# A slot-attention stage in which the context sums, the context norms and one wait change their beats

## What is computed

```python
Pn = rmsnorm(P, input_norm_w)                 # P is the context
k_proj = Pn @ Wk.T
v_proj = Pn @ Wv.T
for _ in range(NUM_ITERS):                    # 3
    sn = rmsnorm(slots, slot_norm_w)
    scores = einsum('bkd,bmd->bkm', sn @ Wq.T, k_proj) * SCALE
    attn = softmax(scores, axis=-2)
    attn = attn / (sum(attn, axis=-1, keepdims=True) + EPS)
    updates = einsum('bkm,bmd->bkd', attn, v_proj)
    slots = gru_cell(updates, slots, ...)
```

## Time and profile before

| | |
|---|---|
| time, median of 3 runs | 1770.23 us (1766.69 to 1775.06) |
| the profiled execution's own time | 1769.67 us |
| its span in the trace | 1767.5 us |
| slot stage, groups 0 to 6 and the start of 7 | 956.45 to 1516.51 us |
| PE busy over the span | 1515.3 us (86%) |
| DVE, POOL, ACT busy over the span | 1294.7, 1207.3, 1080.5 us |

### The profile page before, as it was taken

One profiled execution on the slowest core, in us unless ns is written; L12 is line 12 of the kernel. 1 busy time (PEld: TensorE's weight loads), 2 busy tenths in 40 slices (PEclk: granted clock), 3 DMA queues, 4 the chain that ended last, 5 costly groups with the idle time before them and its releaser, 6 DMA issues. The chain is left out here.

```text
span 1767.5 us, 21744 instructions
## 1 busy us (share of the span) xinstructions
PE 1515.3 (86%) x6178; PEld 899.8 (51%) x6178; DVE 1294.7 (73%) x2194; ACT 1080.5 (61%) x2151; POOL 1207.3 (68%) x863
## 2 busy tenths in 40 slices
PE   4798889988899888898875999999999998918994
PEld 1333334333334333343323676767767776718994
DVE  1999999999999999999970556556566565533552
ACT  3767777777777777777644655456565555303553
POOL 1899999999999999999972134544545444352665
PEclk8889999999999999999897999899999999758997
DMA  4454545455454454454416320202212000007771
GB/s 141 130 167 157 158 154 166 165 161 162 145 174 158 153 170 150 162 172 144 167 39 222 128 90 24 109 17 101 83 41 110 13 1 13 7 18 206 214 204 55
DMA packets 105848, 214.19 MB, mean 121 GB/s; under 512 B 12162, under 2 KB 56709, under 8 KB 105744
## 3 DMA queue, kind: packets, MB, share of 16 engines
q1 hardware_dynamic: 101200, 204.50, 35.6%
q0 software_dynamic: 4544, 8.47, 1.4%
HBM read 168.28 MB, written 45.56 MB: 121 GB/s over the span
## 5 line engine op out<-in xcount | busy, mean ns | idle before, releaser
L321 POOL TENSOR_TENSOR hc<-state,c_rows 128x1024 f32<-128x1024 f32 x256 | 598.9, 2359 | 41.9 <-DVE state L503 35.9
L606 PE MATMUL ps_y<-hc,ident 128*128 128x512 f32 x1024 | 516.2, 647 | 91.0 <-POOL hc L321 91.0
L503 DVE TENSOR_TENSOR_SCAN state<-ps_da,inp 128x512 f32<-128x512 f32 x512 | 590.3, 1199 | 0.0
L395 ACT ACTIVATE ps_da<-dt,a_neg 128x512 f32<-128x512 f32 x512 | 349.1, 688 | 172.4 <-DVE state L503 168.4
L606 PEld LDWEIGHTS ps_y<-hc,ident 128*128 128x128 f32 x1024 | 203.2, 204 | 381.2 <-issue 232.1
L492 DVE TENSOR_TENSOR inp<-dtx,ps_b 128x1024 f32<-128x1024 f32 x192 | 230.7, 1202 | 35.5 <-ACT ps_b L401 19.2
L918 POOL TENSOR_TENSOR rs<-ms,m_half 128x4 f32<-128x4 f32 x48 | 49.5, 1032 | 275.7 <-DVE ms L1144 275.6
L308 POOL TENSOR_TENSOR inp<-dtx,b_rows 128x1024 f32<-128x1024 f32 x64 | 150.8, 2357 | 0.0
L552 PE MATMUL ps_misc<-x1T,w_conv 128*128 128x512 f32 (+3 forms) x256 | 118.9, 609 | 23.1 <-ACT x1T L346 15.3
L401 ACT COPY ps_b<-b_rows 128x512 f32<-128x512 f32 x192 | 111.6, 581 | 26.4 <-DVE inp L492 24.6
L1149 DVE TENSOR_TENSOR sc<-sc,ps_s 77x512 f32<-77x512 f32 x48 | 32.8, 683 | 115.1 <-PE ps_s L1340 115.1
(11 more groups left out here) (210 smaller groups left out, 2736.0 us busy)
## 6 DMA issues: line engine op xcount, KB each, us to landing
b_rows<-bc_rows SPq DMA_DIRECT2D x128, 512.0 KB, 4.8
c_rows<-bc_rows SPq DMA_DIRECT2D x128, 512.0 KB, 4.0
sorted_x<-pad_rows SPq DMA_DIRECT2D x8, 4160.0 KB, 13.5
w<-in_L_ffn_W SPq DMA_DIRECT2D x78, 256.0 KB
xrow<-sorted_x SPq DMA_DIRECT2D x39, 130.0 KB
x_tok<-in_x SPq DMA_DIRECT2D x16, 256.0 KB, 4.5
ctx<-in_ctx SPq DMA_DIRECT2D x16, 154.0 KB
out_x<-orow,target POOLq DMA_INDIRECT x78
```

Source lines behind the costliest of these rows:

```text
L321: pool.tensor_tensor(hc[:, n % RING], state[:, n % RING], over_c(c_rows[:, slot, n % 2]), ALU.mult).then_inc(hc_ready, 1)
L395: act.activation(ps_da[u % DA_RING][:], dt[:, par, c], ACT.Exp, scale=a_neg[:, c, n:n + 1]).then_inc(da_ready, 1)
L503: dve.tensor_tensor_scan(state[:, n % RING, c], ps_da[u % DA_RING][:], inp[:, n % RING, c], 0.0, ALU.mult, ALU.add).then_inc(state_ready, 1)
L606: ins = pe.matmul(ps_y[:, c], ident[:], hc[:, n % RING, c], start=False, stop=n == NS - 1)
```

## The change

The sums of a context are split: `sum_ctx` gets a list of batches, and two of the four are done in each of two beats, in front of the score copy rather than behind it. The sums for lane 1 of the next group stand in beats 0 and 1, those for lane 0 of the group after that in beats 2 and 3. POOL's `norm_ctx` moves from beat 1 to beat 2 (in front of `normed`), and from beat 5 to beat 4 (in front of `labels`). On PE the wait for the copy of "v13" moves from the end of beat 5 to the front of beat 1 of the next group; at the end of beat 5 stands, between `ssq` and `scores`, a wait for the copy of "K1".

```diff
@@ POOL
-                if beat == 1 and not last:
+                if beat == 2 and not last:
                     norm_ctx(i + 1, 1)
                 if beat in (2, 3) and not first:
                     normed(beat - 2, i - 1)
-                if beat == 5 and not last and not (isinstance(i, int) and i == NQ - 2):
+                if beat == 4 and not last and not (isinstance(i, int) and i == NQ - 2):
                     norm_ctx(i + 2, 0)
@@ ACT
-        def sum_ctx(q, k, before):
+        def sum_ctx(q, k, before, batches=range(GB)):
             act.wait_ge(ctx_loaded[k], 16 * q + 16)
             need(act, ctx_normed[k], q)
-            for b in range(GB):
+            for b in batches:
...
+                half = range(beat % 2 * 2, beat % 2 * 2 + 2)
+                if beat in (0, 1) and not last:
+                    sum_ctx(i + 1, 1, (i + 1, 0), half)
+                if beat in (2, 3) and not last and not (isinstance(i, int) and i == NQ - 2):
+                    sum_ctx(i + 2, 0, (i + 1, 1), half)
                 if after_this is not None:
                     attention_scores(*after_this[:2])
-                if beat == 0 and not last:
-                    sum_ctx(i + 1, 1, (i + 1, 0))
...
-                if beat == 4 and not last and not (isinstance(i, int) and i == NQ - 2):
-                    sum_ctx(i + 2, 0, (i + 1, 1))
@@ PE
+                if beat == 1 and not first:
+                    pe.wait_ge(u_read, u_value(i - 1, "v13"))
                 if working:
                     gate_x(b, it2, par2, "r")
...
                     c, it3, j3, q3, par3 = after_this
+                    ssq(c, it3, a, it)
                     if beat == 5:
-                        pe.wait_ge(u_read, u_value(i, "v13"))
-                    ssq(c, it3, a, it)
+                        pe.wait_ge(u_read, u_value(i, "K1"))
                     scores(c, it3, par3)
```

## The result

| | before | after |
|---|---|---|
| median, same chip | 1772.64 us (1766.69 to 1782.13, 4 runs) | 1746.38 us (1745.46 to 1748.29, 4 runs) |
| profiled execution, its span | 1769.67, 1767.5 us | 1748.29, 1746.0 us |
| granted clock of PE over the span | 0.919 | 0.925 |

The ratio is 0.9848 with a 95% interval of [0.9802, 0.9895]: faster by 1.5%, about 26 us, where 12 were forecast. By the two profiled executions it is 21.4 us; the other 5 are in executions of which there is no trace. It also scatters less: 2.8 us between the four runs, against 15.4 before.

What follows compares the result with a forecast made beforehand. POOL's queue was taken to set when groups 2 to 6 begin, with PE's wait for v13 a second stall. Gains of 8.0, 5.0 and 0.5 less 1.4 gave 12.1 us, from 1769.67 to 1757.6 us; range 1750 to 1764.5.

Steps and rivals of the forecast that it cites:

- Norm and sums out of beat 5: Beat 5 of groups 1 to 5 becomes like group 6's 12.37 us; 8.0 us taken, upper end 11.1.
- Wait for v13 a beat later: On PE at the end of beat 5, the sum of squares starts 0.72 us earlier in seven groups; 5.0 us.
- A contention that goes: In group 0's beat 5, DVE's df no longer runs while POOL writes pn; 0.5 us gained.
- What is given back: Beat 0 after a late rs is shorter, so five groups lose 0.28 us each again; 1.4 us lost.
- rival B: Removing PE's idle time at group 2's start also removes the clock's fall; 5.1 us more, 1752.5 us, chance 0.17.
- Half sums in front of the score copy: On ACT, two sums need 0.75 us and fit into 1.05 us of idle time; nothing taken.
- E: Rival: half sums don't fit before ACT's score copy, making 26 beats late; slower, 1779 us and more, chance 0.06.
- Norm in beats 2 and 4: On POOL, the moved norm fits in front of beat 3's root with 0.07 us to spare; nothing taken.
- C: Rival: POOL and DVE get in each other's way in the norm's new places; 1763 us, chance 0.17.
- A: The likeliest case, the slot stage's terms as worked out: 1757.6 us, with bounds 1754.5 to 1760, chance 0.48.

Runs made afterwards that it cites:

- e2: The kernel after without its edits on PE, so the wait for v13 stays in front of the sum of squares; 1755.74 us, ratio 0.9911.
- e4: The kernel before with one edit: POOL's context norm in beat 5 stands behind labels and scatter; 1759.46 us, ratio 0.9939.
- e9: The kernel before with lane 0's norm behind labels and scatter in beat 5 and the v13 wait a beat later; 1748.73 us, ratio 0.9881.
- e1: The kernel before with the two PE edits alone, the v13 wait a beat later; 1776.64 us, ratio 1.0038.
- e6: The kernel after with seven scratch roots on POOL before the root ending beat 5, groups 1 to 6; 1783.04 us, ratio 1.0092.
- e3: The kernel before with only lane 0's context moved: norm to beat 4, sums to beats 2 and 3; 1758.45 us, ratio 0.9931.
- e7: The kernel after with each half sum behind the score copy; 1747.17 us, ratio 0.9893.
- e8: The kernel after with all four sums in front of the score copy, in beats 1 and 3; 1752.24 us, ratio 0.9921.
- e10: The kernel before, unchanged, profiled again in one execution; 1771.74 us.
- e5: The kernel after with five scratch roots on POOL before the root ending beat 5, groups 1 to 6; 1750.4 us, ratio 0.9902.

## Why the prediction was wrong

The mechanism was right: POOL's queue held rs, the change frees it, and PE's wait follows. e2, e4 and e9 show both parts. Nearly every row of its last paragraph came: rs 0.25 us behind ms at each group's start, POOL idle before it, no wait of the sum of squares, the score copy at its old distance with 0.33 us to spare. The size was wrong, 12.1 us where the 46 beats show 22.6, and its range was too narrow. Term by term:

| term | taken | in the traces | how |
|---|---|---|---|
| "Norm and sums out of beat 5" | 8.0 | 11.1 | less 12.37, five groups |
| "Wait for v13 a beat later" | 5.0 | 6.1 | 6 x 0.84 + 1.09 (group 1) |
| "A contention that goes" | 0.5 | 0.45 | group 0: 12.37 to 11.08, less 0.84 |
| "What is given back" | -1.4 | -1.4 | beats 0 at the full clock: 11.37 for 11.09 |
| beat 1 of group 0 | none | 1.6 | DVE's df 6.19 us behind rs instead of 7.79 |
| half-clock stretches | none | 4.7 | what is left of the 22.6 |

- **The clock is the step that failed.** It stood as rival B with 0.17, and the likeliest sum held none of it. From beat 1 of group 0 to beat 4 of group 7, the record of the granted clock shows seven half-clock stretches of 3.4 us and one of 13.7 before, and five of 3.4 after. By the beats that hold them against the same beats without, those of before cost 5.3 us for the long one (16.43 against 11.09), 1.2 to 1.7 for four short ones, 0.35 for the one in beat 0 of group 3 and little for the two in beats 5 of groups 3 and 4, under POOL's wait; 0.7 more is the start of the stage's last stretch. That is 12.2. Those of after cost 1.5, three times 1.7 and 0.9, which is 7.4. The long one was the idle time's doing, as far as experiments can say it: long stalls brought stretches of 6.8 to 13.7 us (e1 four of four, e6 six of six), and where the stalls were gone none over 3.4 us came in groups 1 to 6 (after, e2, e3, e4, e7, e8, e9). B's price of 5.1 us for it was near; what the prediction lacked is this loss in the likeliest sum, and any term for the short stretches. I had held against B that group 6, where rs was as late, kept its clock. That is one draw: e10 shows that the same idle time can go either way. The page "TensorE: Matmul & The Clock Gate", Part 1, of the Trainium skill says that the slow clock is the default and activity releases it; these runs agree, and the long stalls of e6 more than the single case that I weighed.
- **"Norm and sums out of beat 5"** should have been 11.1. I took 8.0 because half-clock stretches might come again in beats 5 of groups 3 and 4. In after all six beats 5 have 1.00; the stretches came in beats 0 instead. They are not bound to a place, so they belonged in a term of their own, and not in this one.
- **"Wait for v13 a beat later"** gave 0.84 and not 0.72 a group. The start moved by exactly 0.72 (0.65 for 1.37 us behind "v13"). The other 0.11 goes with the eight matmuls: they take 0.95 us for 1.05, without an idle time in front, and ms follows: 0.98 us behind their start (1306.59 to 1307.57) instead of 1.09. That the missing idle time is what makes them faster is not shown. And the two edits are not independent, which the sum never said: alone the wait is a loss (e1).
- **Beat 1 of group 0** was missed, since I read the sums' place only in full groups, where 1.05 us of idle time cover them. In group 0 a table load of 1.28 us stands behind them on ACT. e3 against e2 prices it at 2.7 us with the clock stretch that goes with it. That stretch came in all six traces with the late gate, where PE stands idle for 1.92 or 1.93 us (before, e1, e3, e4, e9, e10), and in none of the six others, where it is 0.60.
- **"Half sums in front of the score copy"** at nothing was right, and so E was wrong: 0.73 us fit into 1.05. The estimate of what they would cost uncovered was of the right kind: e8 lost 0.43 us in a beat 2.
- **"Norm in beats 2 and 4"** at nothing was right, and C was wrong. It was close: 0.46 us or more left before rs in five groups, 0.16 in group 3. DVE's h took 0.82 instead of 0.69 us in beats 2, under POOL's instructions, and nothing waited for it.
- **The range** ended at B's lower end alone. A's own best time, 1754.5, less B's 5.1 gives 1749.4, and group 0's beat lay outside both.

What stays open is when the other short stretches come. In after four of the five lie in beats 0, of groups 2, 3, 5 and 7 and not of 1, 4 and 6, though PE's longest idle time is 0.81 us in those of groups 1 to 6; e2 and e4 have them in beats 4 and 5 too. No experiment here moved them on purpose, so how much of the 4.7 us is the change's doing and how much the execution's stays open as well: before and e10, the same kernel, differ by 3.7 us over the 46 beats.

## What to carry to other kernels

Where an in-order queue holds an instruction that waits for late data in front of others that are ready, put it last before you thin the work out: e4 did the same work in the same beat, and beat 5 came down from 14.5 to 12.37 us. Take away a wait on the engine that bounds the kernel only when the other engine's queue no longer sets the next round, or it arrives early just to stand still. And price a stall of PE at its own length plus the clock that may go with it, as a range, since one trace doesn't tell which it will be.

## What the hardware showed that I had not expected

- A stall of PE can cost more than itself, and the longer ones did so each time. At the starts of groups idle times of 1.25 us were followed by no long half-clock stretch (four in e5), 1.51 by one, once, 1.89 and 1.90 by one in the six cases of the two traces of before, 2.16 and 2.17 in both, and 2.7 to 3.5 us in all ten of e1 and e6. Such a stretch cost the beat 1.4 to 5.3 us, so that from e5 to e6 11.8 us more of stalls made 21.2 us more of time in the traces' 46 beats, and 32.6 by the medians.
- The same wait removed is worth 9.4 us in one kernel (e2 to after) and minus 6 in another (before to e1), by the medians.
- The first gate of the stage pays 1.28 us for a table load on ACT, and four small sums in front of that load instead of none made DVE's df 1.6 us later, though POOL's pn beside rh has a share in it.
